# Layer norm, turn and modulation of the attention input moved to the close of the step in front, and the first query product to the place of the turn

## The reference, cut to what matters

```python
# layer 0, s = one sequence; layer 1 has the same shape
y = layernorm(x) * (1 + gamma1[s]) + beta1[s]          # the part that the change moves
q, k, v = y @ Wq + bq, y @ Wk + bk, y @ Wv + bv        # layer 1: q and k are rotated
x1 = x + (softmax(q k^T / 4) v @ Wo + bo) * alpha1[s]  # layer 1: no gate
z = layernorm(x1) * (1 + gamma2[s]) + beta2[s]
out = x1 + (gelu(z @ W1 + b1) @ W2 + b2) * alpha2[s]   # layer 1: no gate
```

## Time and profile before

| what | value |
|---|---|
| median of 3 runs | 1841.35 us (1840.35 to 1844.5) |
| profiled execution, device time | 1841.5 us |
| its span, first to last instruction | 1839.7 us |
| PE matmul busy | 1784.3 us, 97% |
| DVE, ACT, POOL busy | 1247.0 us (68%), 1230.2 us (67%), 852.7 us (46%) |
| mean granted TensorE clock | 0.992 |
| chain that ended last | PE 74%, DVE 11%, issue 7%, ACT 2% |

### The profile page before, as it was taken

One profiled execution on the slowest core, in us unless ns is written; L12 is line 12 of the kernel. 1 busy time (PEld: TensorE's weight loads), 2 busy tenths in 40 slices (PEclk: granted clock), 3 DMA queues, 4 the chain that ended last, 5 costly groups with the idle time before them and its releaser, 6 DMA issues.

```text
span 1839.7 us, 41543 instructions
## 1 busy us (share of the span) xinstructions
PE 1784.3 (97%) x12623; PEld 1634.3 (89%) x12623; DVE 1247.0 (68%) x2985; ACT 1230.2 (67%) x2265; POOL 852.7 (46%) x1036
## 2 busy tenths in 40 slices
PE   7799999999999999999999999999999999999998
PEld 6688999888989888999888999999999999999986
DVE  6777676667676667677677766776766776666751
ACT  4466767766776766677657767666767667767663
POOL 2233433333433433433635566555566555566544
PEclk9899999999999999999999999999999999999999
DMA  6545545444544435554453332333332334342320
GB/s 166 144 113 127 126 91 126 105 111 125 128 99 116 113 104 130 127 140 103 116 152 100 91 107 88 105 102 105 89 109 86 107 99 107 82 114 88 96 72 35
DMA packets 330283, 199.93 MB, mean 109 GB/s; under 512 B 160995, under 2 KB 314597, under 8 KB 330213
## 3 DMA queue, kind: packets, MB, share of 16 engines
q1 hardware_dynamic: 330212, 199.06, 41.0%
HBM read 80.98 MB, written 17.33 MB: 53 GB/s over the span
## 4 chain that ended last, share of the span: by engine, by line
PE 74%; DVE 11%; issue 7%; ACT 2%; SPq 2%; POOL 2%; DMA 1%; DVEq 0%; POOLq 0%; ACTq 0%
PE C L977 17%; PE D L1168 16%; PE B L977 9%; PE B L1124 8%; PE A L1091 6%; PE B L1110 4%; PE A L977 4%; PE E L977 4%; DVE mx L1444 3%; PE A L1096 2%; DVE o_sb L1468 1%; DVE exps L1450 1%; PE E L1135 1%; PE E L1043 1%; DVE z_lo L1391 1%
## 5 line engine op out<-in xcount | busy, mean ns | idle before, releaser
L593 POOL TENSOR_TENSOR h_lo<-hact,h_hi 128x512 fp32r<-128x512 f32 x256 | 331.0, 1293 | 234.9 <-ACT h_hi L800 219.8
L1168 PE MATMUL D<-wgt_hi,h_hi 128*128 128x256 f32 x1024 | 263.4, 290 | 0.0
L1091 PE MATMUL A<-k_pad,q_pad 128*128 128x256 f32 x1536 | 256.1, 293 | 5.7 <-DMA q_pad<-q_flat 2.8
L809 ACT COPY probs_turned<-B 128x512 f32<-128x512 f32 x256 | 149.3, 584 | 167.6 <-PE B L1110 167.5
L1168 PE MATMUL D<-wgt_lo,h_hi 128*128 128x256 f32 x1024 | 255.6, 282 | 0.0
L1124 PE MATMUL B<-v_blocks,probs_turned 128*128 128x68 f32 x2048 | 254.3, 271 | 1.3 <-ACT probs_turned L809 1.3
L1124 PEld LDWEIGHTS B<-v_blocks,probs_turned 128*128 128x128 f32 x2048 | 248.7, 192 | 6.5 <-ACT probs_turned L809 2.3
L795 ACT ACTIVATE hact<-C,b_col 128x512 f32<-128x512 f32 x256 | 175.9, 687 | 83.6 <-PE C L977 81.2
L1444 DVE TENSOR_REDUCE mx<-A 128x8 f32<-128x512 f32 x256 | 174.4, 681 | 68.8 <-PE A L1096 41.2
L1091 PEld LDWEIGHTS A<-k_pad,q_pad 128*128 128x128 f32 x1536 | 211.3, 191 | 9.8 <-DMA q_pad<-q_flat 3.5
L804 ACT ACTIVATE exps<-exps 128x512 f32<-128x512 f32 x256 | 161.6, 632 | 84.7 <-DVE exps L1450 82.3
(11 more groups left out here) (141 smaller groups left out, 3874.5 us busy)
## 6 DMA issues: line engine op xcount, KB each, us to landing
k_pad<-k_flat SPq DMA_DIRECT2D x512, 64.0 KB, 2.1
q_pad<-q_flat SPq DMA_DIRECT2D x256, 128.0 KB, 2.4
gates<-gates SPq DMA_DIRECT2D x64, 256.0 KB, 4.5
x_bias<-x_bias SPq DMA_DIRECT2D x32, 512.0 KB, 3.3
rotation<-rotation SPq DMA_DIRECT2D x256, 64.0 KB, 1.9
x_in<-in_x SPq DMA_DIRECT2D x16, 512.0 KB, 4.5
gates<-gated_bias SPq DMA_DIRECT2D x32, 256.0 KB, 4.7
x_res<-in_x SPq DMA_DIRECT2D x16, 512.0 KB, 4.8
```

The source lines that it names most:

```text
L593: pool.tensor_tensor(hb[1][:, m % 2, :], hact[:, m % 2, :], hb[0][:, m % 2, :].bitcast(F32), ALU.subtract).then_inc(h_lo, 1)
L1091: ins = nc.tensor.matmul(dst, qpad[g % 2][:, c, p, b, :, :].rearrange("p x s -> p (x s)"), kpad[g % 2][:, c, q, :, b * S:(b + 1) * S], sta ...
L1168: ins = nc.tensor.matmul(Dk[g // 2][:, (g % 2) * D:(g % 2 + 1) * D], hb[p][:, m % 2, g * P:(g + 1) * P], w_slice(q, W_FF2, D, m, 0, D), st ...
```

## The change

For tiles 0 and 1 nothing changes but the order. For tiles from 2 on, everything from the layer norm to the low part of y is moved one step forward. In step u, tile u+2 is now not only loaded but normalised, turned, scaled, shifted and split, in banks A0 and A1 (before: A0 and B1, one step later). In the place of the turn PE runs `queries_keys(u+1, 0)`, which stood after `back(u-1, 1)`. POOL's `first_rstd` moves up behind `hidden_low(u-1, 2)`. SP's list is the same as before.

```diff
+        def y_soon(u):
+            return known(u) and u < 1
+        def y_bank(tile, pair):
+            return (A[0], B[1] if known(tile) and tile < 2 else A[1])[pair]
...
@@ POOL, behind hidden_low(u - 1, 2)
+                if n is not None and b is not None:
+                    first_rstd(u + 2)
...
@@ ACT, behind hidden_high(u - 1, 3): layer 0
+                if n is not None and b is not None and a == 0:
+                    first_norm(u + 2)
+                    first_columns(u + 2, n)
...
@@ ACT, behind exponential(u, 3, 1): layer 1
+                if n is not None and b is not None and a == 1:
+                    first_norm(u + 2)
+                    first_columns(u + 2, n)
...
@@ ACT, close of the step
+                elif n is not None:
+                    first_high(u + 2, 0)
+                    first_high(u + 2, 1)
...
@@ PE, scores(u, 0, b)
+                if g == 0 and a is not None and not y_soon(u):
+                    pe.wait_ge(y_lo, upto(u + 1, 2, b + 1))
...
@@ PE, behind project(u, 0)
-                if a is not None:
+                if a is not None and y_soon(u):
                     first_turn(u + 1, 0, b)
                     first_turn(u + 1, 1, b)
+                elif a is not None:
+                    queries_keys(u + 1, a, 0, b)
...
@@ PE, behind turn_probs(u, 3, 1)
+                if n is not None and b is not None:
+                    first_turn(u + 2, 0, n)
+                    first_turn(u + 2, 1, n)
...
@@ DVE, behind second_aggregate(u, 1)
+                if n is not None and b is not None:
+                    first_statistics(u + 2)
                 if a == 0:
                     low_qk(u + 1, 0)
+                if n is not None and b is not None and a == 0:
+                    first_aggregate(u + 2)
...
@@ DVE, behind second_aggregate(u, 2), and y_low behind second_aggregate(u, 3)
+                elif n is not None:
+                    for pair in range(2):
+                        y_scale(u + 2, pair)
+                        y_shift(u + 2, pair)
```

More of the change, by code:

```diff
@@ L271, in qk_bank @@
             return (A + B)[i]
-        def y_bank(pair):
-            return (A[0], B[1])[pair]
+        def y_soon(u):
+            return known(u) and u < 1
+        def y_bank(tile, pair):
+            return (A[0], B[1] if known(tile) and tile < 2 else A[1])[pair]
         def pair_of(buf, pair):
@@ L682, in step @@
                     rotated_low(u + 1, 3)
-                if n is not None:
+                if n is not None and b is None:
                     first_rstd(u + 2)
@@ L759, in first_high @@
                 await_(act, pe_v, upto(tile, 2, 0))
-                nc.scalar.copy(pair_of(yb[0], pair), y_bank(pair)[:, :].rearrange("p (c n) -> p c n", c=KC)).then_inc(y_hi, 1)
+                nc.scalar.copy(pair_of(yb[0], pair), y_bank(tile, pair)[:, :].rearrange("p (c n) -> p c n", c=KC)).then_inc(y_hi, 1)
             def second_high(tile, pair):
@@ L858, in step @@
                     hidden_high(u - 1, 1)
-                if a is not None:
+                if y_soon(u):
                     first_high(u + 1, 0)
@@ L893, in step @@
                     high_piece(2, 0, 2)
+                if known(u) and u == NT - 2:
+                    act.wait_ge(mod_done, 32)
+                if n is not None and b is not None and a == 0:
+                    first_norm(u + 2)
+                    first_columns(u + 2, n)
                 if a == 1:
@@ L953, in step @@
                     high_piece(2, 1, 2)
-                if known(u) and u == NT - 2:
-                    act.wait_ge(mod_done, 32)
-                if n is not None:
+                if n is not None and b is None:
                     first_norm(u + 2)
                     first_columns(u + 2, n)
+                elif n is not None:
+                    first_high(u + 2, 0)
+                    first_high(u + 2, 1)
                 if known(u) and u == 0:
@@ L1026, in first_turn @@
                 pe.wait_ge(xn_ready, upto(tile, G, 2 * pair + 2))
-                if attn is not None:
+                if attn is not None and known(tile) and tile < 2:
                     pe.wait_ge(*((s_sub, upto(tile - 1, 2 * G, 5)), (pv_norm, upto(tile - 1, 2 * G, 4)))[pair])
+                elif attn is not None:
+                    pe.wait_ge(s_sub, upto(tile - 2, 2 * G, 7 + pair))
                 for c in range(KC):
                     for g in range(2):
-                        ins = nc.tensor.transpose(y_bank(pair)[:, (2 * c + g) * P:(2 * c + g + 1) * P],
+                        ins = nc.tensor.transpose(y_bank(tile, pair)[:, (2 * c + g) * P:(2 * c + g + 1) * P],
                                                   x_in[:, 2 * pair + g, c * P:(c + 1) * P], ident[:, :])
@@ L1053, in queries_keys @@
                     pe.wait_ge(y_lo, upto(tile, 2, 1))
-                elif attn is None:
+                if attn is None:
                     pass
-                elif i == 1:
-                    pe.wait_ge(s_sub, upto(tile - 1, 2 * G, 6))
+                elif i < 2:
+                    pe.wait_ge(s_sub, upto(tile - 1, 2 * G, 5 + i))
                 else:
@@ L1394, in y_scale @@
             def y_scale(tile, pair):
-                scale_turned(tile, 0, pair, y_bank(pair), pe_yt, mod1_ready, y_scaled)
+                scale_turned(tile, 0, pair, y_bank(tile, pair), pe_yt, mod1_ready, y_scaled)
             def y_shift(tile, pair):
-                shift_turned(tile, 0, pair, y_bank(pair), y_scaled, y_aff)
+                shift_turned(tile, 0, pair, y_bank(tile, pair), y_scaled, y_aff)
             def y_low(tile, pair):
-                low_turned(tile, pair, y_bank(pair), yb, y_hi, y_lo)
+                low_turned(tile, pair, y_bank(tile, pair), yb, y_hi, y_lo)
             def z_scale(tile, pair):
@@ L1631, in step @@
                     cosine(u + 1, 0)
+                if n is not None and b is not None and a == 1:
+                    first_aggregate(u + 2)
+                if a == 1:
                     sine(u + 1, 1)
@@ L1694, in step @@
                     second_aggregate(u, 3)
+                if n is not None and b is not None:
+                    y_low(u + 2, 0)
+                    y_low(u + 2, 1)
                 if known(u) and u == NT - 1:
```

1 line of the change is left out of this document (removed).

## The result

The changed kernel takes 1918.7 us (median of five runs, 1916.6 to 1920.3) against 1842.1 us of the kernel before in the same comparison: a ratio of 1.041, interval 1.040 to 1.043. It is slower by 77 us; forecast were 1919 us. The profiled execution has a span of 1918.5 us, 78.8 more than before, and a mean granted clock of 0.984.

A forecast was written before the change was run, and what follows sets the result against it. PE, busy 97% of the span, was taken as the bound, so only its waits count. Layer 0 +35, layer 1 +33, steps 1 and 30 -2, clock +12: together +78 on 1841.5, giving 1919 us, range 1858 to 1957.

The forecast's parts named there:

- Layer 0, 14 x 2.5: Layer 0 steps: late load, statistics, norm and table load delay `turn_probs(u,3,0)`; +2.5 a step in 14 steps, 35 us.
- forecast 1.8: Layer 0: `turn_probs(u,3,0)` starts at 566.6 instead of 564.80, 1.8 later in the step.
- forecast 0.7: Two turns of four transposes, 2 x 0.35, come back later in the same step; also the gain if nothing else waits.
- third query product: Layer 0: waits for a normalisation, starts near 560.3 instead of 559.4, so PE reaches `turn_probs(u,3,0)` near 564.1.
- Layer 1, 15 x 2.2: Layer 1 steps: DVE's wait for the load holds up the rotation; +2.2 a step in 15 steps, 33 us.
- the forecast 0.4: Layer 1: the later turn of heads delays low part, output, store and load, adding 0.4 to the step.
- Clock, +12: Layer 0: PE's waits of about 2.5 us halve the clock in half of 14 steps, at 1.7 each: +12 us.
- the rival's 1955: Rival: the clock falls in every layer 0 step, up to 48 us more, 1955 us; chance 0.12.
- The ends, -2: Steps 1 and 30 only gain, together -2 us.
- `y_low`, which the prediction had taken at 0: First score product of a step might wait for `y_low`; given 0 to 0.3 a step, taken as 0.
- the 8 that is subtracted: Subtracted in the range's lower bound, layer 0 at +1.8 and layer 1 at nothing: 1841.5 + 25 - 8 = 1858 us.
- the load is in time: Rival: `x_in` lands early enough, only the gain of about 0.7 a step in 30 steps remains, 1820 us; chance 0.09.

The follow-up runs named there:

- a_early: The early load: the changed kernel with SP's load of `x_in` issued ahead of its wait for the output of tile u-2; 1826.9 us, ratio to before 0.991.
- the doses: Two runs of the changed kernel with `x_in`'s load issued ahead of the copy into `x1m` (1918.6 us) or right behind the store (1845.7 us).
- the table and the order runs: Changed kernel with layer 0's table load ahead of `first_norm` (1893.0 us), or with norm, statistics or `first_rstd` moved later, singly or combined (1852.0 to 1919.5 us).
- a_shift: The changed kernel with the early load and the new order beginning with tile 3 instead of tile 2; 1825.6 us, ratio 0.991.
- a_stat: The changed kernel with layer 1's statistics and aggregates put behind sine and cosine of chunk 1, layer 0 as it is; 1919.5 us, ratio 1.041.
- a_ahead: The changed kernel with the load of `x_in` issued just ahead of the copy into `x1m`, still behind the store's landing; 1918.6 us, ratio 1.041.

## Why the prediction was right

**The mechanism was the forecast one, link by link.** In us into the step of layer 0, forecast and measured: landing 29.1 and 29.3, first `low_qk` 30.4 and 30.6, norm 33.7 and 34.0, `turn_probs(u,3,0)` 39.5 and 39.6, PE there from 37.0 and 37.2, its wait 2.5 and 2.47. In layer 1 the first rotation stood at 34.8 and 35.1, `turn_probs(u,3,0)` at 39.3 (39.7 with the later start) and 39.8, the wait was 1.5 and 1.3 to 1.4. The early load shows that all of it hangs on the landing, the doses show a price of one for one, and the table and the order runs show that it goes through the links named.

**Layer 0, 14 x 2.5.** The steps of the loop without a fall of the clock grew by 2.8. In the step above `turn_probs(u,3,0)` starts 39.64 us into the step where it was 37.73, 1.9 later (forecast 1.8), and what comes behind it takes 17.96 where it took 17.12, 0.84 more (forecast 0.7). The 0.6 to 0.8 ahead of the third query product, which the prediction saw as a later arrival, adds nothing: PE would only have waited longer at `turn_probs`.

**Layer 1, 15 x 2.2.** Steps 19 to 29 grew by 2.2 to 2.4; the load is issued 24.95 us into the step where it was 24.55, the forecast 0.4. That a second list, POOL's, would have held the rotation up by itself was not in the prediction: it took `first_rstd` to be over before the swap lands, which holds in the changed kernel (it starts at 1349.37 and takes some 2.1, against 1352.10) but not once the sine is freed. Steps 15 to 17, around the change of layer, grew by 1.8 us together in place of 6.6.

**Clock, +12.** It fell in seven of the steps 2 to 14, as half of 14 steps were taken to. In four of them (3, 4, 7, 11) it fell behind the wait at `turn_probs`, as forecast; these took 58.9 to 59.1, some 1.4 more. In the steps 2, 13 and 14 it fell 34 to 35 us into the step, ahead of `turn_probs` and behind shorter waits, which the prediction did not have, so that the count agrees is partly luck. Seven times 1.4 is about 10. Windows of the changed kernel behind the wait of 2.49 in step 3 and behind that of 2.47 in step 9:

```profile
247.60:251.20 3.60, 3.60 (x14) 3.08 (x13) 1.07 (x4) 2.48 (x4) 0.00 (x0) 0.53 0.00 0
...
596.80:600.20 3.40, 3.40 (x25) 3.01 (x25) 2.24 (x6) 2.55 (x4) 0.00 (x0) 1.00 0.00 0
```

In the first PE ran at 1.2 GHz for nearly all of 3.6 us, in the second at 2.4. "TensorE: Matmul & The Clock Gate" of the Trainium skill, section "HAM oscillation — how this bites in real kernels", speaks of a throttle in each turn of such a loop. Here the clock fell in four of the ten steps 3 to 12, and the rival's 1955 did not come.

**The ends, -2, and step 0.** Step 1 gained 0.7 and step 30 1.0, as forecast. The step that was wrong is step 0, which the prediction counted among the 14 of layer 0 at 2.5: it grew by 6.1, from 54.2 to 60.4. As the change of order begins with tile 2, step 0 turns and modulates two tiles, tile 1 in the old order and tile 2 in the new (16 transposes of `x_in` and four `y_low` in its trace, eight and two before). PE's first scores of step 1 wait for `y_low`, which the prediction had taken at 0:

```profile
92.25 1.62 PE L1110 MATMUL A<-k_pad,q_pad 128*128 128x256 f32 x6 [2.44 <-DVE y_lo L1415]
```

Besides, the clock stood at 0.50 for 21.9 us of step 0 where it was 15.7. `a_shift` shows that DVE's one-time work is not the whole of it, for the doubled step costs 3.8 in step 1 too; how the 6.1 divide was not tested.

**The sum.** Steps 0, 1 and 30 +4.5, steps 2 to 14 +46.2, steps 15 to 29 +28.6, together 79.2 (what lies ahead of step 0 and behind step 30 gives 0.4 back). The 14 steps of layer 0 came to 52.3 against 35 + 12, layer 1 to 28.6 against 33: errors of 5 and 4 in opposite directions. That the sum came out within a microsecond is chance. In the lower bound of the range, the 8 that is subtracted is worked out nowhere; with the forecast gain of 0.7 in 15 steps of layer 1 and the ends it would be 12.5.

**What was only partly seen** is the way out: the rival "the load is in time" was given 1820, and with the load moved the kernel runs in 1826.9.

## What to carry to other kernels

Before work is moved a step forward, look where its input lands in that step, and then at what stands behind each of its consumers in every in-order list: the work itself was free here, the wait in front of it held up three engines. Moving the load ahead of an unrelated wait on the queue was worth more than mending the orders one after the other, since each mended order only handed the wait to the next. When a step of a loop shows a wait with two possible holders, remove both before judging either.

## What the runs showed that was not expected

Two transfers of 512 KB that are issued close together both take longer. In steps 19 to 29 of layer 1 the load takes 3.7 to 4.2 us and the copy 3.0 when they are 11.6 us apart (`a_early`); 4.0 to 4.1 and 3.2 to 3.3 when the load comes 1.0 behind the copy (the changed kernel); 4.2 to 4.9 and 5.0 to 5.7 when the load comes 0.44 ahead of the copy (`a_ahead`). So of the 0.57 us that `a_ahead` issued the load sooner, only 0.1 was left at the landing.

The clock does not follow the length of a wait alone. Behind 1.35 us of waiting in `a_stat` it was halved in that step, behind 1.32 at the same place of the changed kernel it was not; the windows of the one, then of the other:

```profile
1353.80:1357.20 3.40, 3.40 (x11) 2.82 (x12) 1.65 (x4) 3.08 (x6) 2.67 (x3) 0.53 0.31 94
```

```profile
1356.80:1360.20 3.40, 3.40 (x24) 3.01 (x24) 2.99 (x6) 3.06 (x7) 2.67 (x3) 1.00 0.45 112
```

What tells such steps apart is left open.
